# Token score operands laid out in quarters of 32 rows, score maxima issued in groups of four, shift rows written by GpSimd's queue, and value writes with runs twice as long

## The reference

```python
query = hidden_states @ Wq;  keyt = enc @ Wk;  valt = enc @ Wv
hs = _mha(query, keyt, valt)                            # 8 heads, softmax over 2044 keys
ca_q1 = jnp.einsum('btc,th->bch', ca, Wq_ca)            # 384 x 640: rank 4 in the tokens
ca_q1 = ca_q1[:, indices, :]                            # 384 rows gathered to 1024
ca_hs1 = _mha(ca_q1, residual, residual)                # keys and values are x itself
ca_hs2 = _mha(ca_hs1 @ Wq, ca @ Wk_ca, ca @ Wv_ca)      # softmax over the 4 tokens
out = (hs + ca_hs2) @ Wout + b_out + residual
```

## Time and profile before

| | |
|---|---|
| time, median of 3 runs | 1229.41 us |
| the profiled execution's own time | 1230.95 us |
| its span | 1229.1 us |
| PE busy | 1215.3 us (99%) |
| PEld (weight loads) busy | 957.6 us (78%) |
| DVE busy | 827.8 us (67%) |
| ACT busy | 678.5 us (55%) |
| POOL busy | 205.4 us (17%) |
| granted TensorE clock | 9 tenths or more in every slice |

### The profile page before, as it was taken

One profiled execution on the slowest core, in us unless ns is written; L12 is line 12 of the kernel. 1 busy time (PEld: TensorE's weight loads), 2 busy tenths in 40 slices (PEclk: granted clock), 3 DMA queues, 4 the chain that ended last, 5 costly groups with the idle time before them and its releaser, 6 DMA issues.

```text
span 1229.1 us, 14526 instructions
## 1 busy us (share of the span) xinstructions
PE 1215.3 (99%) x5644; PEld 957.6 (78%) x5644; DVE 827.8 (67%) x1168; ACT 678.5 (55%) x773; POOL 205.4 (17%) x114
## 2 busy tenths in 40 slices
PE   7999999999999999999999999999999999999999
PEld 6889988898667677777777777777777777776899
DVE  6348824592244378878878778878888888885552
ACT  5232424222544466677677677677677677778310
POOL 1100000001000011222312322221221221221233
PEclk9999999999999999999999999999999999999999
DMA  8995898896650063254254254244344335322264
GB/s 296 272 332 190 214 291 236 285 286 148 215 134 1 1 193 92 70 151 108 66 151 108 81 135 108 94 122 109 108 117 115 102 107 138 120 89 65 68 212 150
DMA packets 96720, 180.68 MB, mean 147 GB/s; under 512 B 17306, under 2 KB 50330, under 8 KB 92523
## 3 DMA queue, kind: packets, MB, share of 16 engines
q1 hardware_dynamic: 88938, 157.33, 46.6%
q0 software_dynamic: 2816, 11.80, 3.1%
q10 hardware_dynamic: 4896, 10.62, 2.5%
HBM read 116.32 MB, written 63.24 MB: 146 GB/s over the span
## 4 chain that ended last, share of the span: by engine, by line
PE 97%; DMA 2%; ACT 1%; SPq 0%; issue 0%; DVE 0%; ACTq 0%
PE at_ps L1231 29%; PE at_ps L1212 19%; PE bank L652 18%; PE at_ps L210 9%; PE acc_t_ps L1008 7%; PE at_ps L1418 6%; PE s_ps L975 2%; PE bank L629 2%; DMA q_lo_d<-out_lo 1%; PE bank L599 1%; PE f_ps L948 1%; PE acc_t_ps L986 1%; PE f_ps L210 1%; PE f_ps L927 1%; PE f_ps L937 0%; DMA ctx_f<-in_ctxT 0%
## 5 line engine op out<-in xcount | busy, mean ns | idle before, releaser
L218 DVE TENSOR_REDUCE mpart<-at_ps 128x1 f32<-128x512 f32 x480 | 326.3, 686 | 109.9 <-PE at_ps L210 108.3
L1153 ACT ACTIVATE prob_hi<-at_ps 128x1024 fp32r<-128x1024 f32 (+1 forms) x256 | 263.1, 1028 | 194.5 <-PE at_ps L1212 194.5
L1231 PE MATMUL at_ps<-prob_hi,v 128*81 128x512 f32 (+1 forms) x1024 | 318.8, 396 | 0.2 <-issue 0.2
L1090 DVE TENSOR_TENSOR prob_lo<-probs,prob_hi 128x1024 fp32r<-128x1024 f32 (+1 forms) x211 | 270.8, 1283 | 23.5 <-ACT probs L1158 23.4
L1158 ACT ACTIVATE probs<-at_ps 128x1024 f32<-128x1024 f32 (+1 forms) x256 | 261.1, 1020 | 0.0
L1231 PEld LDWEIGHTS at_ps<-prob_hi,v 128*81 128x81 f32 (+1 forms) x1024 | 153.8, 151 | 59.5 <-issue 6.1
L1090 POOL TENSOR_TENSOR prob_lo<-probs,prob_hi 128x1024 fp32r<-128x1024 f32 x45 | 108.0, 2401 | 519.7 <-ACT probs L1158 519.7
L210 PE MATMUL at_ps<-a 128*128 128x512 f32 x480 | 194.2, 405 | 0.0
L210 PEld LDWEIGHTS at_ps<-a 128*128 128x128 f32 x480 | 153.7, 320 | 31.9 <-DVE mpart L218 0.8
L1212 PE MATMUL at_ps<-a 128*128 128x512 f32 (+1 forms) x512 | 161.5, 396 | 1.2 <-ACT probs L1158 0.6
L1212 PE MATMUL at_ps<-b 113*128 113x512 f32 (+1 forms) x512 | 160.5, 394 | 0.0
(11 more groups left out here) (144 smaller groups left out, 1420.7 us busy)
## 6 DMA issues: line engine op xcount, KB each, us to landing
v_hi_d<-v_t SPq DMA_DIRECT2D x16, 648.0 KB, 9.2
v_lo_d<-v_t SPq DMA_DIRECT2D x16, 648.0 KB, 12.5
v<-v_hi_d SPq DMA_DIRECT2D x16, 648.0 KB, 4.9
v<-v_lo_d SPq DMA_DIRECT2D x16, 648.0 KB, 6.0
k_hi_d<-out_hi SPq DMA_DIRECT2D x40, 256.0 KB, 6.1
k_lo_d<-out_lo SPq DMA_DIRECT2D x40, 256.0 KB, 7.2
a<-k_hi_d SPq DMA_DIRECT2D x16, 640.0 KB, 7.2
b<-k_hi_d SPq DMA_DIRECT2D x16, 640.0 KB, 11.2
```

The lines of the kernel that those rows point to most:

```text
L218: dve.tensor_reduce(self.mpart[:, g % 2, qt, c:c + 1], mx_ps[k % 2][:, 0:w], AX, ALU.max).then_inc(self.mx_done, 1)
L1090: eng.tensor_tensor(pl[n % PB][0:r, :], prob[n % PF][0:r, :], ph[n % PB][0:r, :].bitcast(F32), ALU.subtract).then_inc(sem, 1)
L1153: act.activation(ph[n % PB][0:r, :], s_ps[n % 2][0:r, :], ACT.Exp, scale=SCALE).then_inc(ph_done, 1)
L1231: mm = pe.matmul(o_ps[:, u * CH:(u + 1) * CH], a[0:r, t, :], y[n % PB][0:r, u * CH:(u + 1) * CH], start=t == 0 and m == 0, stop=t == KT - ...
```

## The change

- `u` gets 128 rows: head h has 16 of them, from row 32 (h mod 4) + 16 (h div 4): 4 high, 4 high, 4 low, one of ones, 3 of zeros. `ca` has the same rows and, for each batch, only 2 x 384 columns (heads 0 to 3 and heads 4 to 7), both batches loaded and split once. The split uses columns of per-row factors (`marks`).
- A token score matmul contracts over the 32 rows of its head's quarter only. The maxima come in groups of 4 heads, one for each quarter, into four banks. The 24 groups stand beside the second chunk's q jobs, the third chunk's k and v jobs and one k job of the last chunk (`GROUPS_AT`).
- `u2` and `ca2` are copies of `u` and `ca` turned by 64 rows, made by DMAs within SBUF on the SP queue. Of a pair of score matmuls in `tokens` one uses `u`, `ca` and the other `u2`, `ca2`, so that they lie in different quarters.
- Batch 0's second load and split of `ca` in `tokens` go. All shift rows (2 batches x 8 heads x 2 copies) are written by GpSimd's queue.
- `v_t`'s halves hold 4 heads and four 128-row blocks each, so a run is 4 x 81 floats, 1296 bytes. The v jobs run over all blocks of one half of the heads and then of the other.

The diff, cut to its core:

```diff
-CA_PARTS = 4
+GROUPS_AT = {("q", 1): (0, 1, 2, 3, 4), ("k", 2): (0, 2, 4), ("v", 2): (1, 4, 7), ("k", 3): (1,)}
+def token_row(h):
+    return 32 * (h % 4) + 16 * (h // 4)
+def token_columns(h):
+    return slice(h // 4 * CD, (h // 4 + 1) * CD)
+def quarter(h, turned=False):
+    q = (h + 2 * turned) % 4
+    return slice(32 * q, 32 * (q + 1))
...
+        def with_maxima(some, c):
+            for i, job in enumerate(some):
+                jobs.append(job)
+                if i in GROUPS_AT.get((job[0], c), ()):
+                    top, kc, u = maxima.pop(0)
+                    jobs.extend(("m", u, (4 * top + r, kc, u)) for r in range(4))
...
-                    if c == 1:
+                    if b == 0 and c == 1:
                         pool.wait_ge(w_lo, 3)
-                        pool.wait_ge(ca_lo, b + 1)
-                        pool.dma_start(ca_f[0:K3, None, 0:NH * CD], d["caBD"].rearrange("b k n -> k b n")
-                                       [:, bass.ds(b, 1), :]).then_inc(ca_in, 16)
-            pool.wait_ge(top_done, 2 * B)
-            shift_tokens(pool, kept, ca, B - 1, range(1, NH, 2))
+                        pool.dma_start(ca_raw, d["ca_rows"].rearrange("b k n -> k b n")).then_inc(ca_in, 16)
+            pool.wait_ge(kept["ca2_in"], 32)
+            for b in range(B):
+                pool.wait_ge(top_done, 2 * (b + 1))
+                shift_tokens(pool, kept, b)
+        def turn(sp, to, a, columns, sem):
+            for half in range(2):
+                rows, from_rows = slice(64 * half, 64 * half + 64), slice(64 - 64 * half, P - 64 * half)
+                sp.dma_start(to[rows, columns].bitcast(F32), a[from_rows, columns].bitcast(F32)).then_inc(sem, 16)
...
-                    if b == B - 1 and n == last_m + 2:
-                        sp.wait_ge(top_done, 2 * B)
-                        shift_tokens(sp, kept, ca, b, range(0, NH, 2))
+                    if (kind, c, m) == ("k", NQ, 0):
+                        sp.wait_ge(done, b * NJ + last["u", NQ - 1] + 1 + 8)
+                        turn(sp, u2, u_all, slice(b * SQ, (b + 1) * SQ), kept["u2_in"][b])
+                        if b == 0:
+                            sp.wait_ge(ca_lo, 1)
+                            turn(sp, ca2, ca, slice(0, B * 2 * CD), kept["ca2_in"])
...
-                        sp.wait_ge(ca_lo, B + 1)
-                        sp.dma_start(kept["ca_f"][0:K3, 0:NH * CD], d["caBD"][0]).then_inc(kept["ca0_in"], 16)
...
-                            sp.dma_start(to[bass.ds(b * NH, NH), :, at:at + 2 * DA].rearrange("h p n -> p h n"),
-                                         v_t[:, i, half].rearrange("p h t d -> p h (t d)")
+                            sp.dma_start(to[some, :, at:at + CH // P * DA].rearrange("h p n -> p h n"),
+                                         v_t[:, i, u].rearrange("p h t d -> p h (t d)")
...
-                        at = hc // KC * CD + hc % KC
-                        pe.matmul(bank[:], ca[0:K3, at:at + (P - 1) * KC + 1:KC],
-                                  u_all[0:K3, bass.ds(b * SQ + u * CH, CH)], start=True, stop=True
+                        at = b * 2 * CD + token_columns(h).start + kc
+                        pe.matmul(bank[:], ca[quarter(h), at:at + (P - 1) * KC + 1:KC],
+                                  u_all[quarter(h), bass.ds(b * SQ + u * CH, CH)], start=True, stop=True
...
-    for h in some:
-        row = ca[K3:K3 + 1, h * CD:(h + 1) * CD].rearrange("o (p c) -> o p c", c=KC)
+    for h in range(NH):
+        for i, ca in enumerate((kept["ca"], kept["ca2"])):
+            r = quarter(h, i == 1).start + 16 * (h // 4) + 3 * NT
...
                 for t in range(2):
-                    st = 2 * j + t
-                    mm = pe.matmul(s_ps[k % 2][:, t, 0:CD],
-                                   kept["u"][0:K3 + 1, b * SQ + st * P:b * SQ + (st + 1) * P],
-                                   ca[b][0:K3 + 1, h * CD:(h + 1) * CD], start=True, stop=True)
+                    st, rows = 2 * j + t, quarter(h, t == 1)
+                    mm = pe.matmul(s_ps[k % 2][:, t, 0:CD], u[t][rows, b * SQ + st * P:b * SQ + (st + 1) * P],
+                                   ca[t][rows, col:col + CD], start=True, stop=True)
```

More of the change, by code:

```diff
@@ L304, in project @@
         stages = [("wk", flat[:, 0:n_k]), ("wv", flat[:, n_k:2 * n_k]),
-                  ("wqca", flat[:, 2 * n_k:2 * n_k + MC * K3]), ("wq", ca_f[:])]
+                  ("wqca", flat[:, 2 * n_k:2 * n_k + MC * P]), ("wq", ca_f[:])]
         stages = [(n, v.rearrange("p (m n) -> p m n", m=w[n][0].shape[1])) for n, v in stages]
-        jobs, maxima = [], [("m", 0, (hc, u)) for hc in range(NH * KC) for u in range(2)]
-        for c in range(NS):
[L311 to L316, removed]
+        jobs = []
+        maxima = [(top, kc, u) for u in range(2) for top in range(NH // 4) for kc in range(KC)]
+        def with_maxima(some, c):
[4 more added lines that the diff above has]
+                    jobs.extend(("m", u, (4 * top + r, kc, u)) for r in range(4))
+        for c in range(NS):
+            with_maxima([("k", c, m) for m in range(MC)], c)
+            with_maxima([("v", c, (t, u)) for u in range(2) for t in range(4)], c)
             if c < NQ:
-                jobs += [("q", c, m) for m in range(MC)] + [("u", c, 0)]
+                with_maxima([("q", c, m) for m in range(MC)], c)
+                jobs.append(("u", c, 0))
         assert not maxima
@@ L324, in project @@
         last = {(kind, c): n for n, (kind, c, _) in enumerate(jobs)}
-        last_m = last["m", 0]
+        last_m = last["m", 1]
         def read_ctx(c):
@@ L494, in scalar @@
                     elif kind == "u":
[L495 to L496 removed]
+                        if b == 0 and c == 0:
+                            act.wait_ge(marks_in, 16)
+                        dst = u_all[:, bass.ds(b * SQ + c * CH, CH)]
+                        act.activation(dst, banks[n % 8][:], ACT.Identity, bias=marks[:, 2:3], scale=marks[:, 0:1]
+                                       ).then_inc(hi_done, 1)
                     else:
@@ L511, in split_x, with split_ca @@
                 dve.tensor_tensor(lo[:], x_f[:, 0], hi[:].bitcast(F32), ALU.subtract).then_inc(x_lo, 1)
[L513 to L517, removed]
+            def split_ca():
+                dve.wait_ge(ca_hi, 1)
+                dve.scalar_tensor_tensor(out=ca[:], in0=ca_f[:, 0:B * 2 * CD], scalar=marks[:, 4:5],
+                                         in1=ca[:].bitcast(F32), op0=ALU.mult, op1=ALU.add).then_inc(ca_lo, 1)
             def negate_top(b):
@@ L559, in vector @@
                         split_x(b, 1)
-                    if kind == "q" and m == 0 and c == 1:
-                        split_ca(b)
+                    if b == 0 and kind == "q" and m == 0 and c == 1:
+                        split_ca()
                     bank = banks[n % 8]
                     if kind == "m":
-                        hc, u = m
+                        h, kc, u = m
                         dve.wait_ge(full, b * NJ + n + 1 + NJ)
-                        dve.tensor_reduce(part[:, hc, u:u + 1], bank[:], AX, ALU.max).then_inc(done, 1)
+                        dve.tensor_reduce(part[:, h * KC + kc, u:u + 1], bank[:], AX, ALU.max).then_inc(done, 1)
                         if n == last_m:
@@ L576, in vector @@
                     elif kind == "u":
-                        dst = u_all[2 * HT:K3, bass.ds(b * SQ + c * CH, CH)]
-                        dve.tensor_tensor(dst, bank[2 * HT:K3, :], dst.bitcast(F32),
-                                          ALU.subtract).then_inc(done, 1)
+                        if b == 0 and c == 0:
+                            dve.wait_ge(marks_in, 16)
+                        dst = u_all[:, bass.ds(b * SQ + c * CH, CH)]
+                        dve.scalar_tensor_tensor(out=dst, in0=bank[:], scalar=marks[:, 1:2], in1=dst.bitcast(F32),
+                                                 op0=ALU.mult, op1=ALU.add).then_inc(done, 1)
                     else:
@@ L1444, in program @@
             "small_in": s.sem("small_in"),
-            "ca0_in": s.sem("ca0_in"),
+            "u2_in": [s.sem(f"u2_in{b}") for b in range(B)],
+            "ca2_in": s.sem("ca2_in"),
             "xn1_in": [s.sem(f"xn1_in{j}") for j in range(ST // 2)],
```

116 lines of the change are left out of this document (55 added, 61 removed).

## The result

The changed kernel takes 1234.74 us (median of 14 runs, 1230.15 to 1240.22) against 1230.34 us of the kernel before in the same comparison (14 runs, 1228.95 to 1234.49). The forecast was 1210 us, faster. The measured time lies inside the stated range (1200 to 1238 us), but it moved the other way. The runs fall into two kinds: five with a granted TensorE clock of 1.0, at 1230.15 to 1230.83 us, and nine with a mean clock of 0.990 to 0.997, at 1233.3 to 1240.2 us. So there are two results to explain: why there is no gain at full clock, and why the clock falls. The profiled execution is of the second kind (span 1237.5 us).

A forecast was written before the change was run, and what follows sets the result against it. TensorE, busy for 99% of the span, was taken as the bound. Gains of 17.4 - 24 E (maxima) and 11.3 - 64 E (scores), with E = 0.106, gave 19.4 us: 1230.95 to 1211.5, or 1210.0 us as median; range 1200 to 1238.

The forecast's parts named there:

- 28.7 - 88 E: Total gain in us: maxima 17.4 - 24 E plus token scores 11.3 - 64 E, E paid at each visit.
- The overlap: Matmuls in different quarters stream at once: a group of maxima costs 0.233 us + E, a score pair 0.178 + E.
- Rival 2: Weight loads of groups and pairs run one after another: gains of only 5.1 and 4.5 us, 1219.8 us; chance 0.15.
- E: Extra cost of each visit to the 32-row layout, taken as 0.106 us for maxima and scores alike.
- rival 1: Each layout change empties the array, at 88 visits: decides from E = 0.33; 1229.7, 1245 or 1262 us; chance 0.20.
- What I called 0: Value writes' gain of 0 to 1.5 us and VectorE's lag, set against each other and both called 0.
- the stall behind a DMA: TensorE lost 1.5 us in all behind ScalarE waiting for a ring slot; 0 to 1.5 us to be won.
- VectorE's lag: Reductions of the maxima fall 1.2 us behind in one place: cost 0, at most 1.2 us a batch.
- The split of `ca`: Ahead of the first q's eviction, some 1.48 + 1.76 us: just hidden; if not, a few tenths, once.
- The queues: SP's copies and GpSimd's 32 shift DMAs stay hidden; without cover the first score would wait some 6 us.
- rival 3: DMA becomes the bound of the projections: a loss of up to 6.4 us, 1216.4 us; chance 0.10.
- Rival 4: Matmuls in different quarters run one after another at no extra cost: 1229 us; chance 0.05.

The follow-up runs named there:

- e2: Changed kernel with both score matmuls of a pair in the same quarter: 1245.67 us, ratio 1.012.
- e8: e3 with the second score matmul of each pair in its quarter, the first over 128 rows: 1243.14 us, ratio 1.0105.
- e4: e3 with the maxima contracted over all 128 rows too, so no matmul in quarters is left: 1226.31 us, ratio 0.9975.
- e5: Kernel before with only the longer value runs and the v jobs' order that goes with them: 1228.46 us, ratio 0.999.
- e1: Changed kernel with token scores contracted over all 128 rows (different result), maxima still in quarters: 1220.6 us, ratio 0.9926.
- e7: Changed kernel with the first six token pairs in quarters, the other 58 over all 128 rows (different result): 1221.42 us, ratio 0.9953.
- e3: Changed kernel with `ca` block diagonal over 8 x 384 columns, token scores over 128 rows, maxima in quarters, no turned copies: 1219.5 us, ratio 0.9922.

## Why the prediction was wrong

**What bounds the kernel** was right: TensorE throughout, and matmuls priced by their columns. So was the form of the sum, 28.7 - 88 E.

**The overlap** was right, and better than the value I took for it: the loads of a group run at once, partners cost nothing (e2: 0.17 us for the lack of it). Rival 2, loads one after another, is out.

**E, the extra cost of a visit, failed.** I took the step of an uncovered load, 0.106 us, "for both kinds". It is 0.35 us at the scores (e8, and 1.82 - 1.29 - 0.178) and 0.455 at the maxima (e4). The reason I gave, that the second matmul's load would be late, wasn't even the mechanism. What costs is the change of layout: the array runs empty or nearly so, and loads stand in the open, on both sides, which is rival 1. I had its point of decision (0.33 us) and gave it 0.20. Its three prices were 0.33, some 0.5, and 0.67 and 0.78 us; the measured ones lie between the first and the second. The rows pointed to it: nothing in them showed that a load for a quarter can go ahead of a full matmul, and I let the rule for equal layouts stand for unequal ones. By measured values the sum is 17.4 - 24 x 0.455 = +6.5 at the maxima and 11.3 - 64 x 0.35 = -11.1 at the scores, -4.6 together, 1234.0 us. The Trainium skill, TensorEngine Tiling (Array Packing), Tiling Modes, gives a drain of TensorE for a change of tiling mode and none for a change of tile within one. These runs agree: the first load of a group starts 0.32 us after the last full matmul, and the four loads in four quarters take 0.26 us together.

**What I called 0** was some 4 us: 1234.0 by the sum, 1230.3 measured at full clock (4.6 if the sum starts from the 1230.34 us of the same comparison). The value runs give 1.0 us (e5), the maxima's new places and rows some 2 (e4 against e5); the stall behind a DMA is gone. The remaining 1 to 1.6 us is in the token stage, which lost 8.7 to 9.7 us (e1) and not 11.1. The six visits in the opening are part of it: in e7's trace, at full clock, the token stage is only 0.25 us longer than in e1's, not 1.0. VectorE's lag cost nothing: of the chain from 60 to 274 us TensorE's matmuls make up 99.8%. The split of `ca`, "just hidden; if not, a few tenths, once", held TensorE up for 0.47 us ahead of the first group (74.39 to 74.86 us; the view names no releaser, but VectorE's part of the split ends at some 74.7).

**The queues** were right: the first token score starts 0.24 us after the last v matmul (274.50 after 274.26 us), so no shift row was late, and rival 3 is out: the projections took 10.5 us less without a wait for a DMA. Rival 4 is out by e2.

**The clock** was not in the prediction at all. It turns "no change" (1230.3) into slower (1234.74). I had looked at the full clock in every slice of the kernel before and asked nothing of what the change would do to it. That 1234.74 lies inside the range of 1200 to 1238 is luck: the range reached that far for rival 1's sake, and the number comes of an E more than three times mine, some 4 us that I had at 0, and the clock.

## What to carry to other kernels

Matmuls in different row quarters run side by side with their loads, but a visit from and back to full-height matmuls costs 0.35 to 0.46 us here (no run has another height, such as 64 rows). So four of 512 columns gain (0.94 to 0.69 us) and two of 384 lose (0.355 to 0.53): count what stands in a visit, not the rows that are saved. An operand laid out in quarters and block diagonal can serve both ways, and e3, which does so, is the version to keep, at 1219.5 us.

## What the runs showed of the hardware

- A lone matmul over 32 rows among full ones adds 0.35 us to a step (e8); inside a visit, four strided loads of 0.25 us take 0.26 together.
- TensorE's granted clock can fall to its lower level in a stretch where TensorE looks busy (5.00 of 5.00 us in the stretches above) when that work is small matmuls, switches and short waits; it fell in 9 of 14 runs of the changed kernel, so a single profile can show either. Look at the mean clock of every run before comparing medians.
- Longer runs of value writes, 1296 instead of 648 bytes, took a v write's landing from 12.5 to 7.3 us (e5, where they are the change, with the v jobs' order), and were worth 1.0 us.
- The same first 45 matmuls took 11.83 to 13.29 us from trace to trace, with the granted clock at 1.00 from 7 us on in all. The reason is open; a difference of 1 us between two traces can come from there alone.
